# Modulation and weight loading cut into single steps with places of their own, and a third buffer for weight pieces

## The reference

```
x = L0(x, c)   # DiT block: modulated LN, attention (16 heads of 9, q and k normed with gains), MLP 144-576-144
x = L1(x, c)   # x + ((x U) R - x U) U^T, U = qr(P), R = expm(A(silu(c) W^T + b)), one 64x64 rotation per sequence
x = L2(x, c)   # DiT block, no norm of q and k
x = L3(x, c)   # DiT block; the MLP is a mixture of 4 experts, top 2 by softmax gate
mod = silu(c) @ w_mod + b_mod ; shift, scale, gate = split(mod, 6)   # in layers 0, 2, 3
x = x + gate * attention(LN(x) * (1 + scale) + shift); the same form for the MLP
```

## Time and profile before

| | us |
|---|---|
| median of 3 runs | 1465.5 (1464.52 to 1466.96) |
| the profiled execution, its own time | 1456.89 |
| its span, first to last instruction | 1455.1 |
| PE busy in it | 1341.2 |
| mean granted clock of PE | 0.965 |

### The profile page before, as it was taken

One profiled execution on the slowest core, in us unless ns is written; L12 is line 12 of the kernel. 1 busy time (PEld: TensorE's weight loads), 2 busy tenths in 40 slices (PEclk: granted clock), 3 DMA queues, 4 the chain that ended last, 5 costly groups with the idle time before them and its releaser, 6 DMA issues. The chain is left out here.

```text
span 1455.1 us, 35686 instructions
## 1 busy us (share of the span) xinstructions
PE 1341.2 (92%) x13526; PEld 1073.8 (74%) x13526; DVE 955.0 (66%) x2914; ACT 946.4 (65%) x1904; POOL 516.5 (35%) x574
## 2 busy tenths in 40 slices
PE   6588999999898999989999999999999999999998
PEld 2356777677777776667777777778888888888897
DVE  4378878888887647778778777844645545454431
ACT  2264777877777646678776667685667575767642
POOL 3363868879875321212222222210211111111010
PEclk9698999999999999999999999999999999999999
DMA  5221000000000001031000000000000101010000
GB/s 150 64 58 24 9 15 15 11 15 15 11 16 17 17 5 40 17 87 42 17 19 20 20 18 18 20 9 6 23 11 19 23 6 23 7 22 8 20 5 21
DMA packets 54527, 34.96 MB, mean 24 GB/s; under 512 B 8240, under 2 KB 52059, under 8 KB 54230
## 3 DMA queue, kind: packets, MB, share of 16 engines
q1 hardware_dynamic: 54358, 32.68, 9.7%
HBM read 28.10 MB, written 2.99 MB: 21 GB/s over the span
## 5 line engine op out<-in xcount | busy, mean ns | idle before, releaser
L1670 PE MATMUL p_B<-s_pC,s_H 128*128 128x144 f32 x1900 | 250.4, 287 | 1.7 <-DVE s_ON L1290 0.6
L1670 PEld LDWEIGHTS p_B<-s_pC,s_H 128*128 128x128 f32 x1900 | 238.8, 190 | 7.3 <-issue 1.2
L1271 DVE TENSOR_REDUCE s_MX<-p_S 128x16 f32<-128x2048 f32 x96 | 219.4, 2285 | 12.9 <-PE p_S L1585 12.2
L860 POOL TENSOR_TENSOR s_X<-s_X,s_GA 128x144 f32<-128x144 f32 x96 | 48.1, 502 | 451.1 <-DVE s_GA L1296 450.9
L991 ACT ACTIVATE s_Pm<-p_S 128x2048 f32<-128x2048 f32 x96 | 180.3, 1878 | 19.2 <-PE p_S L1599 18.3
L856 POOL TENSOR_TENSOR s_s<-s_s,s_half 128x32 f32<-128x32 f32 x32 | 174.8, 5464 | 29.2 <-DVE s_s L1239 29.1
L1043 ACT ACTIVATE s_H<-p_B,s_pC 128x512 f32<-128x512 f32 (+1 forms) x216 | 142.9, 690 | 56.1 <-PE p_B L1521 54.3
L1527 PE MATMUL p_B<-s_eye,s_QK 128*128 128x128 f32 x768 | 117.6, 282 | 9.7 <-DVE s_GA L1296 2.6
L1527 PEld LDWEIGHTS p_B<-s_eye,s_QK 128*128 128x128 f32 x768 | 87.5, 143 | 28.0 <-issue 9.0
L870 POOL TENSOR_TENSOR s_X<-s_X,s_GM 128x288 f32<-128x288 f32 x48 | 39.1, 814 | 186.2 <-DVE s_GM L1377 114.7
L1521 PE MATMUL p_B<-s_XMh,s_WFh 128*128 128x512 f32 x216 | 100.0, 463 | 5.1 <-DVE s_QK L1258 3.8
(11 more groups left out here) (308 smaller groups left out, 3224.2 us busy)
## 6 DMA issues: line engine op xcount, KB each, us to landing
s_GA<-gates SPq DMA_DIRECT2D x96, 72.0 KB, 2.9
s_GM<-gates SPq DMA_DIRECT2D x48, 144.0 KB, 3.3
s_QT<-s_MS SPq DMA_DIRECT2D x192, 8.0 KB
s_SG<-in_main SPq DMA_DIRECT2D x33, 72.0 KB, 2.0
out<-s_X SPq DMA_DIRECT2D x8, 288.0 KB, 2.7
s_RW<-in_rotw SPq DMA_DIRECT2D x8, 256.0 KB
s_SGS<-in_mains SPq DMA_DIRECT2D x33, 45.0 KB, 2.4
s_pC<-in_pack SPq DMA_DIRECT2D x1, 1450.0 KB, 8.8
```

What stands on the lines that cost most here:

```text
L860: e.tensor_tensor(X[:, n % B, :], X[:, n % B, :], GA[n % NGA][:], ALU.add).then_inc(SEM["xa"], 1)
L1271: e.tensor_reduce(MX[n % 2][:, :], bank["s1", i][:, :].rearrange("p (h k) -> p h k", h=NH), AX.X, ALU.max, negate=True).then_inc(SEM["mx"], 1)
L1670: ins = e.matmul(bk[:, 256 * i2:256 * i2 + C], H[k % 2][0:n, c, 128 * t:128 * t + 128], w2[l][0:n, 5 * x + c, :], start=(c == 0), stop=(c ...
```

## The change

The step `mod` becomes mw (the load, SP), ma and mc (one half's product on PE and its copy on ACT), ms (copies to MRS, DVE), mo (the transposes, PE, with a bank of its own), mv (moves to MT, DVE) and mg (store of the gates, SP). The step `wt` becomes wd (a piece's two DMAs, SP), wc (the centring, DVE), wt (the casts, ACT) and wl (the low part, DVE). The loads of pP and pC are pk, of the later parts of X xl, of eye2 and ltm el. No step has a wait behind its first instruction, except on products of its own. There are three buffers SG instead of two (NSG). Layer 3's wait for the end of the rotation (early_end) stays at pk and moves from the pieces' DMAs to their casts. MIXED keeps `rt` alone. The dry run now lets DMAs share one queue of 170 bytes per ns, with 550 ns an issue and 2000 ns to land. All places are new numbers.

```
-NGA = 3
+NGA, NSG = 3, 3
-MIXED = ("mod", "wt", "rt")
+MIXED = ("rt",)
-LAND, LOAD, TURN = 2200, 1300, 60
+LAND, LOAD, TURN = 2000, 1300, 60
+RATE = 170
...
+            if e == "sp":
+                queue = max(queue, now) + parts[e][s][k].size / RATE
-                events.append((now + (LAND if parts[e][s][k].table == "dma" else HOP[e]), count, e, x))
+                events.append(((queue + LAND if e == "sp" else now + HOP[e]), count, e, x))
...
-    put(-9.0, "mod", 0)
-    for j in range(last_piece(0, "q") + 1):
-        put(-8.5 + 0.1 * j, "wt", j)
...
+    for l in LAY:
+        s = START[f"mod {l}"]
+        put(s - 1.5, "mw", l)
+        for hf in range(2):
+            put(s + 0.1 * hf, "ma", l, hf)
+            put(s + 0.1 * hf + 0.05, "mc", l, hf)
+        for k, stage in enumerate(("ms", "mo", "mv")):
+            put(s + 0.2 + 0.05 * k, stage, l)
+        put(s + START["gates"], "mg", l)
+    def pieces(l, part, s, step):
+        first = min(j for j, p in enumerate(PIECES) if p[0] == l and p[1] == part)
+        put(s - 0.3, "pk", l, part)
+        for j in range(first, last_piece(l, part) + 1):
+            put(s + step * (j - first) - START["piece"], "wd", j)
+            for k, stage in enumerate(("wc", "wt", "wl")):
+                if stage != "wc" or j < 2:
+                    put(s + step * (j - first) + 0.05 * k, stage, j)
...
-        SG, SGS = sb("SG", [128, 2, SGC]), sb("SGS", [80, 2, SGC])
+        SG, SGS = sb("SG", [128, NSG, SGC]), sb("SGS", [80, NSG, SGC])
...
+                elif stage == "wd":
+                    j = i[0]
+                    l, part, c0, c = PIECES[j]
+                    k = j % NSG
+                    if j >= NSG:
+                        w.wait_ge(*at("wl", j - NSG))
...
+                elif stage == "pk":
+                    l, part = i
                     if l == 3:
                         w.wait_ge(*early_end)
...
+                    if l == 3:
+                        w.wait_ge(*early_end)
                     e.copy(W_[0][:, r], SG[:, k, 0:c]).then_inc(SEM["wh"], 1)
...
+                if stage == "ma":
+                    l, hf = i
+                    wm = MODS[l][0]
+                    w.wait_ge("sil", 2)
+                    w.wait_ge(f"d_mod{l}", 32)
+                    bk = take(stage, i)
+                    c = slice(432 * hf, 432 * hf + 432)
+                    e.matmul(bk[0:32, 0:432], sT1[:, :], wm[0][:, c], start=True, stop=False)
+                    e.matmul(bk[0:32, 0:432], sT2[:, :], wm[1][:, c], start=False, stop=True).then_inc(SEM["mod_mm"], 1)
```

More of the change, by code:

```diff
@@ L69, in freed_by @@
     return FREED[stage], i
-def uses(step):
-    return 2 if step[0] == "mod" else 1
 def bank_kind(stage):
@@ L232, in plan @@
     work, slow, window = deque(), 2, WINDOW
-    gap = None
+    gap, queue = None, 0.0
     def met(waits):
@@ L267, in begin @@
         kind = bank_kind(s[0]) if e == "pe" else None
-        for k in range(uses(s) if kind else 0):
-            use = (s[0], s[1] + (k,)) if s[0] == "mod" else s
+        if kind:
             if kind == "S":
-                bank[use] = tuple(idle["S"])
+                bank[s] = tuple(idle["S"])
                 idle["S"].clear()
             else:
-                bank[use] = (idle["B"] or idle["S"]).popleft(),
-            before[use] = {last[b] for b in bank[use] if b in last}
-            held.setdefault(s if s[0] in IN_PLACE else freed_by(*s), []).append(use)
+                bank[s] = (idle["B"] or idle["S"]).popleft(),
+            before[s] = {last[b] for b in bank[s] if b in last}
+            held.setdefault(s if s[0] in IN_PLACE else freed_by(*s), []).append(s)
         return True
@@ new lines @@
+START = {"layer 2": 4.243, "layer 3": 5.169, "mlp": (2.607, 2.762, 3.223), "mlp last": (-0.176, 2.665, 2.748),
+         "mlp step": (4.102, 2.127, 3.832), "rot": 3.495, "rot step": 0.644, "qr": -0.019, "qr step": 0.475, "e1": -6.545,
+         "e1 step": 0.266, "e2": 1.332, "e3": -4.124, "e5": 4.205, "e6": 3.42, "sq": 6.443, "sq step": 1.461, "q1": -0.155,
+         "q2": -2.585, "switch": 1.892, "lend": 0.655, "mod 0": -13.465, "mod 2": 2.553, "mod 3": 2.698, "gates": -1.996,
+         "piece": 0.303, "wq 0": -12.216, "wf 0": -0.324, "wf step": 0.944, "wq 2": 6.633, "wf 2": 2.875, "wq 3": 1.492,
+         "x": -9.434, "x step": 0.044}
@@ L385, in n_pos @@
         return n + (0.0, START["layer 2"], START["layer 3"])[n // B]
-    put(-9.0, "mod", 0)
-    for j in range(last_piece(0, "q") + 1):
-        put(-8.5 + 0.1 * j, "wt", j)
-    for j in range(last_piece(0, "q") + 1, last_piece(0, "f") + 1):
-        put(0.5 + 0.3 * (j - 3), "wt", j)
-    put(2.0, "mod", 2)
-    put(3.0, "mod", 3)
-    for j in range(last_piece(0, "f") + 1, last_piece(2, "q") + 1):
-        put(6.0 + 0.3 * (j - 8), "wt", j)
+    for l in LAY:
[15 more added lines that the diff above has]
+                    put(s + step * (j - first) + 0.05 * k, stage, j)
+    pieces(0, "q", START["wq 0"], 0.1)
+    pieces(0, "f", START["wf 0"], START["wf step"])
+    pieces(2, "q", START["wq 2"], 0.3)
+    for k in range(1, 4):
+        put(START["x"] + START["x step"] * k, "xl", k)
+    put(START["x"] + 2 * START["x step"], "el")
     for u in range(NA // 2):
@@ L447, in order @@
             if m == NG - 1:
-                for j in range(last_piece(2, "q") + 1, last_piece(2, "f") + 1):
-                    put(p + 2.4 + 0.2 * (j - 11), "wt", j)
-                for j in range(last_piece(2, "f") + 1, len(PIECES)):
-                    put(s + 1.5 + 0.3 * (j - 16), "wt", j)
+                pieces(2, "f", p + START["wf 2"], 0.2)
+                pieces(3, "q", s + START["wq 3"], 0.3)
+                pieces(3, "f", s + START["wq 3"] + 0.9, 0.3)
     for k in range(D):
@@ L905, in scalar_program @@
                         w.wait_ge(*at("mod_rs", 1))
-                    for hf in range(2):
-                        w.wait_ge("mod_mm", 2 * k + hf + 1)
-                        e.copy(MODS[l][1][:, 432 * hf:432 * hf + 432], bank["mod", (l, hf)][0:32, 0:432]).then_inc(SEM["mod_cp"], 1)
+                    e.copy(MODS[l][1][:, 432 * hf:432 * hf + 432], bank["ma", i][0:32, 0:432]).then_inc(SEM["mod_cp"], 1)
                 elif stage == "wt":
@@ L1038, in scalar_program @@
                     else:
+                        w.wait_ge("d_gs0", 16)
                         w.wait_ge("d_gs3", 16)
@@ L1150, in vector_program @@
             for stage, i in steps["dve"]:
-                if stage == "mod":
+                if stage == "ms":
                     l = i[0]
```

170 lines of the change are left out of this document (81 added, 89 removed), and 12 rows, old and new, of the table TILE.

## The result

| | before | after |
|---|---|---|
| median of four runs each, us | 1465.5 (1464.5 to 1467.0) | 1423.8 (1412.8 to 1438.6) |
| ratio | | 0.969, 95% interval 0.962 to 0.976 |
| profiled execution, us (span) | 1456.9 (1455.1) | 1438.6 (1436.7) |
| predicted | | 1441.5, range 1428 to 1458 |

The account below looks back on a forecast made before the run. The prediction took PE as the bound, held up at the start by X loads, a weight piece, ACT's in-order casts and layer 2's modulation. Its terms, -20 - 4 = -24, took 1465.5 to 1441.5 us, range 1428 to 1458.

Parts of the forecast that it names:

- The bound and the chain: Start: X loads, weight piece, ACT's in-order casts and layer 2's modulation hold up PE; layer 3 is pure PE work.
- Part 1: Start: layer 0's QKV products go ahead of layer 2's matmuls, first score product at 46.6 instead of 82.3; -20 us net.
- second rival: Start and layer 3: fillers at full rate (4) and router's less crowded place (7) save more; 1430.5 us, chance 0.15.
- first rival: Layer 0 eats the head start as tiles queue at POOL; -10 in all, 1455.5 us, chance 0.17.
- Part 2: Layer 3's weights near 620 us: WQ pieces loaded early, gelus ahead of WF's first cast; -4 us, bounds 0 and -6.
- Part 3: 44 more fillers, DMA issues, moved waits and other new places cost nothing: 0, within 8 us each way.
- Part 4: Layer 3's clock: the drop behind the router's matmuls should stay; 0, between -7 and +5 us.
- the slow rival: Layer 3's repeated group: a new wait and clock fall, 4 us in each of eight groups; 1473.5 us, chance 0.07.
- The sum and the base: Whole kernel: -20 - 4 = -24 us, taken from the median of the runs shown, 1465.5, giving 1441.5.
- The clock helps as well: Start and layer 3: fillers at full rate (4), router's drop halved (7); -35 in all, 1430.5 us, chance 0.15.
- A new wait in layer 3's group: Layer 3: a step waits on DVE's maximum and the clock falls, 4 us per group; +8, 1473.5 us, chance 0.07.
- it does not do what it says: Start: first QKV product waits for X or mod 0's DMA, 15 of the 20 us go; 1465.5 us, chance 0.06.

Follow-up runs that it names:

- e3: Changed kernel's order up to the first score product of tile 8, the old order behind it; median 1430.3 us, ratio 0.981 to the kernel before.
- e2: Changed kernel's code with every engine's order as it was before the change; 1464.1 us, ratio 1.002 to the kernel before.
- e6: Changed kernel with layer 3's router products set apart, pair by pair, ahead of up or projection products; 1421.6 us, ratio 0.970 to the kernel before.
- e9: Changed kernel with layer 3's router pairs set apart, also ahead of the MT transposes, so sooner than in e6; 1412.0 us, ratio 0.963.
- e4: Changed kernel's order up to the first score product of tile 64, the old order behind it; 1434.6 us, ratio 0.977 to the kernel before.
- e7: Changed kernel without any of its 182 filler matmuls; 1455.0 us, ratio 0.990 to the kernel before.
- e1: The changed kernel run again with no edit; median 1427.8 us, ratio 0.972 to the kernel before.

## Why the prediction was wrong, point by point

**The bound and the chain** were read rightly. The wait at modulation 2's transposes is gone, the first QKV product began at 28.7 (27 to 32 forecast), the first score product at 43.2 (42 to 50), PE is busy for 29 of 30 to 60 us.

**Part 1, the start, -20 with bounds -12 and -27: this step failed.** It is the term that was sized too small: the start is worth -31 by mean spans (e3 against e2), or -28 by e3's ratio to the kernel before. Of its terms, "32 fillers take 12 us" at 0.38 each measured 10.7 (5.49, 1.83, 2.50 and three in 0.83), since they ran at full rate from 22 us on; 31.4 became 28.7 and 46.6 became 43.2. That is 3 us, the first half of my second rival. By that rival's rule the first QKV product would have waited for data alone; it waited 0.36 us. The Trainium skill (TensorE: Matmul & The Clock Gate, What's actually happening) says that the clock is throttled by default and activity releases it; the fillers' 0.46 and then 0.25 us agree with it, but the first twelve still ran at the low rate.

The rest is a term that I had put at nothing: I priced the head start in PE work "at full clock" and in waits, and left the clock of the first 200 us as it was. Up to tile 8 e2 loses 22.2 us to the clock. PE idles at half clock for 11.9 us there, so 6 of the 22 are waits that my sum had. e6 and e9, the changed kernel's start without the long stretch, lose 6.8 and 5.1, and are 28 to 29 us ahead of e2 at tile 8. With the stretch the lead is 1 to 12 us (187.1, 180.1 and 176.7 against 188.5). So the head start has no one value; my 20 lay between the two, and e3's 21.2 in one profile is luck in part. That layer 0 would keep what is there at tile 8 was right: 21.2 us at tile 8 and 22.2 at tile 64 (e3 against e2's 888.5), so the first rival fell: where the head start shrinks, it is to the clock and not to POOL.

**Part 2, layer 3's weights, -4.** The 5.17 us wait of ACT at the first cast of WF is gone; PE's idle around it fell by 1.3 us over 580 to 660. The whole middle is worth 3 by mean spans (e4 against e3) and 9 in the two profiles, with 12 less lost to the clock between tile 8 and tile 64. The forecast lies between; that this wait gave it is not shown.

**Part 3, fillers and other places, 0.** It was wrong about the fillers as a class: "Cover gone, they cost 44 x 0.19 = 8 us" looked only for a cost. All together they buy 27 us (e7). What the 44 new ones bring by themselves wasn't tried. It was wrong about layer 3 too, whose new places give some 5 us apart from the clock, 3 of them PE's waits.

**Part 4, the clock in layer 3, 0 between -7 and +5.** Within its bounds, but not 0: from tile 64 on the loss to the clock fell from 17.4 to 19.3 us to 12.6 to 14.5, 3 to 7 less. "The drop should stay" was right for nearly every group, but two or three of the drops had been twice as long (6.8 us), and none in e1 is, after 950 us. In 1000 to 1400 the clock is 0.98 instead of 0.97. The period is 68.1 us for the four tiles behind tile 88, from 68.9, below the 69 at which the slow rival would have set in.

**The sum and the base.** -31, -3 and -7 add up to the -41 between e2 and e1 because they are steps of one chain; over all runs the change is worth 36 us by means and 32 by medians. I carried the sum over to a median of 1465.5 that was 5 us above what 73 more runs gave. And I gave the time a range without asking whether the changed kernel would have one time: with 10 of 16 executions above 1427 and 6 under 1421, which median four runs give is luck.

**The rivals.** *The clock helps as well* (1430.5, 0.15) was right in kind. Its first half named the fillers' rate (3 us) and missed what hangs on the stretch of 45 to 110 us; its second half put 7 us on the router's place, where 3 to 7 were measured for the clock of all of layer 3. *A new wait in layer 3's group* and *it does not do what it says* found nothing.

**What stays open:** why the clock stays low for 31 to 61 us although PE is busy all the time, what decides between two executions of one program, and whether the start's fillers, the modulation's or the chip change how often the long one comes.

## What to carry to other kernels

Take the spread and the granted clock of several runs before pricing a change by one profile, and split each run into span times clock and the rest; the rest overstates what the clock costs wherever PE waits or another engine sets the pace. Time a stage by itself too, from a first instruction to a last: layer 3's hardly varied while the whole varied by 30 us, and only that told what the order and the router's products were worth. Filler products pay where a stage has gaps, and do nothing ahead of a first product that waits for data. Where PE "busy" consists of products with few columns, the clock may fall behind it; putting those products apart took the drops away here, and not the time, since the new spacing cost as much.

## What the runs showed of the hardware

- Two issues of loads of GM from 26.05 on in the changed kernel hold SP's queue for 5.33 us together, as one behind X did for 5.13 at 30.20 before; no wait of PE for a load behind them is among its longest.
